# The input laid out a second time by features and normalised there, in place of transposes on TensorE

## Chip, cores and metric

One core of a Trainium2 chip runs the whole program. The metric is the device time of one execution in microseconds (us). A run's time is given as the median of several executions; the profile comes from one more execution, whose own time is given beside it. Engines are named as the profile names them: PE is TensorE's matmul side and PEld its weight loads, DVE is VectorE, ACT is ScalarE, POOL is GpSimd, SP (SPq for its queue) is SyncE, which here only issues DMAs.

## What is computed

The input x has 8 batches of 2048 tokens of 512 features. The reference, cut to what matters:

```python
    def proj(W, b):
        y = jnp.einsum('nse,fe->nsf', x, W) + b
        return y.reshape(n, s, h, d).transpose(0, 2, 1, 3)
    ...
    scores = jnp.einsum('nqhd,nkhd->nhqk', Q, K) * scale
    attn = jax.nn.softmax(scores, axis=-1)
    out = jnp.einsum('nhql,nlhd->nqhd', attn, V)
    out = out.reshape(n, s, e)
    return jnp.einsum('nse,fe->nsf', out, Wo) + bo
...
x = x + _layernorm(_L0_attn_ref(_layernorm(x, axis=-1), ...), axis=-1)
x = x + _layernorm(_L0_ffn_ref(_layernorm(x, axis=-1), ...), axis=-1)
```

By the order of the axes the attention runs, at each position, among its 16 heads of 32 features: 16 queries on 16 keys. Of the second block both kernels compute the row-wise part: a layer norm of a layer norm of x (statistics B), gain and shift (`ln_g`, `ln_b`), a layer norm (statistics C) and the residual; the contribution of its gathered attention is left out. Everything is float32, and each projection is computed with operands split in a high and a low part (`w_hi`, `w_lo`, `xT_hi`, `xT_lo`), as three products hi*hi + lo*hi + hi*lo.

## The kernel before

The tokens are cut into 128 tiles of 128 tokens (`NT`), and two tiles are a pair (`NV` = 64 pairs). All engines run the same loop over slots `s` (-4 to 135). In slot `s` PE computes, in this order: the transposes of x of tile s+1 (line 527, four 128 x 128 blocks of `xn` into the PSUM bank `ps_tv`), the scores of tile s-1 (line 554, 32 small matmul pairs), the context of tile s-2 (line 570), the projections K, Q and V of tile s (line 534, 12 matmuls each), and the output projection Y of tile s-2 (line 604). V goes into the same bank `ps_tv` that the transposes use.

There is no scheduler. The order on every engine is the order in which the lines are written, and engines wait for each other with counting semaphores.

What stands around the change:

- **x in.** SP loads `x_in` (tokens on partitions) a pair at a time. DVE takes its statistics (`x_moments`, lines 313 to 317), POOL the root of the variance (`root("X", v)`), ACT the shift (`shift("X", v)`), and ACT writes the normalised row `xn` (line 452, `normalise`). PE transposes it, ACT rounds it to the high half `xT_hi` (line 456), and DVE forms the low half `xT_lo` (line 329, `x_low`) from `ps_tv` and `xT_hi`. Feature 0 of `xn` is a constant 1, since the first row of the weights is taken out of all others and the bias stands in its place.
- **DVE in a slot.** y plus bias (353), `x_low` of tile s+1, statistics A (361; every other slot their moments), the softmax of tile s-1 (369, 371, 383, 387, 389), `kT` (396, a transpose of K out of PSUM), `pT` (403), then in odd slots the statistics B of a pair and in even slots the statistics C of a pair and those of x, then `qT` (426), and in odd slots z times gain (432).
- **POOL in a slot.** In even slots the root of A, then in every slot the softmax's last factor (266), in even slots x + residual (275), in odd slots the root of B and z + shift (282), in even slots the root of C and the output's residual (288), then the root of x.
- **ACT in a slot.** `xT_hi`, the high half of the context (480), exp (486), `xn`, in even slots the rows of A, then `v_tok` out of `ps_tv` (504), then in odd slots the rows of B into z, in even slots the rows of C into `o_sb`.
- **SP in a slot.** In odd slots the store of a pair of outputs (185), `v_key` of tile s-1 (191), read back from the DRAM scratch `v_d`, four copies `k_bd` of tile s (202), four copies `p_bd` of tile s-1 (213), then in odd slots the load of `x_in` (160), in even slots that of `res` (163), and last the store of `v_tok` of tile s into `v_d` (230). SP waits in this order: a wait that isn't met holds up every DMA behind it.

Statistics names: X for x, A, B and C for the three later layer norms. A pair costs two slots, an even and an odd one.

## Time and profile before

| | us |
|---|---|
| median of 3 runs | 1791.14 (1788.35 to 1793.31) |
| the profiled execution, its own time | 1792.47 |
| its span, as the profile shows it | 1790.9 |
| PE busy | 1720.9 (96% of the span) |
| DVE busy | 1440.6 (80%) |
| ACT busy | 850.9 (48%) |
| POOL busy | 831.5 (46%) |
| DMA, mean share of 16 engines | 54% |

The span is what the profiler's clock shows between first and last instruction; 1.6 us of the execution's own time lie outside it. A timeline row gives the start, the duration, the engine, line, operation and names; in brackets the idle time of that engine just before, and which engine's work ended it. For SPq the duration is the time that the queue took to issue the DMA, not that of the transfer.

### The profile page before, as it was taken

What the parts mean: (1) busy time and instruction counts of PE and PEld (TensorE: products, weight loads), DVE (VectorE), ACT (ScalarE), POOL (GpSimd) and SP (SyncE); (2) the same over time, 40 slices, a digit from 0 to 9 for tenths busy, and PEclk for the clock granted to TensorE, in tenths of its full rate; (3) what the DMA queues carried; (4) which work ended last, traced back from release to release, by engine and by line L of the source; (5) the groups of instructions that cost most, each with busy time, mean ns of one, the idle gap of its engine ahead of it and who ended that gap; (6) DMA issues with size and microseconds to landing.
All of it is one profiled execution on the core that took longest, in us unless ns stands there. A gap on an engine that the chain in (4) does not pass through costs nothing.

```text
span 1790.9 us, 55853 instructions
## 1 busy us (share of the span) xinstructions
PE 1720.9 (96%) x23040; PEld 1391.3 (78%) x23040; DVE 1440.6 (80%) x2824; ACT 850.9 (48%) x1800; POOL 831.5 (46%) x782
## 2 busy tenths in 40 slices
PE   4999999999999999999999999999999999999992
PEld 3778878878888788878887888788878888888771
DVE  6688878878888888878888888788878888888874
ACT  4244444445444444445444444445445445445443
POOL 1144445445444444445445444445445445445445
PEclk9999999999999999999999999999999999999996
DMA  6455555565565555555565565555565565555451
GB/s 205 106 127 136 128 146 142 127 151 138 127 153 137 126 148 142 127 138 150 126 151 134 132 152 139 125 146 145 124 147 142 129 149 136 131 148 139 116 132 59
DMA packets 361267, 244.31 MB, mean 136 GB/s; under 512 B 285875, under 2 KB 285875, under 8 KB 360502
## 3 DMA queue, kind: packets, MB, share of 16 engines
q1 hardware_dynamic: 361014, 240.75, 53.9%
q8 instruction: 182, 2.98, 0.7%
q14 instruction: 71, 0.58, 0.1%
HBM read 106.44 MB, written 67.11 MB: 97 GB/s over the span
## 4 chain that ended last, share of the span: by engine, by line
PE 95%; issue 1%; DVE 1%; POOL 1%; ACT 1%; SPq 0%; DMA 0%; POOLq 0%; ACTq 0%
PE ps_k L534 21%; PE ps_y L604 20%; PE ps_tv L534 20%; PE ps_q L534 20%; PE ps_s L554 6%; PE ps_o L570 5%; PE ps_tv L527 3%; POOL o_sb L288 0%; POOL z L282 0%; POOL x L275 0%; SPq L202 0%; DMA p_bd<-pT 0%; SPq L213 0%; ACT z L447 0%; ACT o_sb L447 0%
## 5 line engine op out<-in xcount | busy, mean ns | idle before, releaser
L266 POOL TENSOR_TENSOR probs<-probs,inv 128x512 f32<-128x512 f32 x128 | 136.0, 1062 | 396.3 <-DVE inv L389 396.3
L504 ACT ACTIVATE v_tok<-ps_tv 128x512 f32<-128x512 f32 x128 | 76.5, 597 | 500.0 <-PE ps_tv L534 500.0
L282 POOL TENSOR_TENSOR z<-z,b_row 128x512 f32<-128x512 f32 x128 | 193.1, 1529 | 226.0 <-DVE z L432 226.0
L432 DVE TENSOR_TENSOR z<-z,g_row 128x512 f32<-128x512 f32 x128 | 88.6, 692 | 169.5 <-ACT z L447 168.5
L288 POOL TENSOR_TENSOR o_sb<-o_sb,x 128x512 f32<-128x512 f32 x128 | 161.2, 1280 | 119.7 <-ACT o_sb L447 119.7
L486 ACT ACTIVATE probs<-probs 128x512 f32<-128x512 f32 x128 | 81.0, 632 | 189.2 <-DVE probs L371 189.1
L275 POOL TENSOR_TENSOR x<-x,res 128x512 f32<-128x512 f32 x128 | 163.0, 1295 | 1.7 <-ACT x L447 1.6
L534 PE MATMUL ps_k<-wk_hi,xT_hi 128*128 128x512 f32 x512 | 154.2, 423 | 3.9 <-DVE wk_lo L325 3.9
L534 PE MATMUL ps_tv<-wv_hi,xT_hi 128*128 128x512 f32 x512 | 142.0, 399 | 7.2 <-DVE xT_lo L329 7.2
L604 PE MATMUL ps_y<-wo_hi,oT_hi 128*128 128x512 f32 x512 | 141.8, 399 | 4.8 <-DVE oT_lo L376 4.8
L604 PE MATMUL ps_y<-wo_hi,oT_lo 128*128 128x512 f32 x512 | 142.4, 400 | 0.0
L534 PE MATMUL ps_k<-wk_hi,xT_lo 128*128 128x512 f32 x512 | 141.7, 398 | 0.7 <-issue 0.7
L604 PE MATMUL ps_y<-wo_lo,oT_hi 128*128 128x512 f32 x512 | 142.1, 400 | 0.0
L534 PE MATMUL ps_k<-wk_lo,xT_hi 128*128 128x512 f32 x512 | 141.0, 397 | 0.6 <-issue 0.6
L534 PE MATMUL ps_q<-wq_hi,xT_hi 128*128 128x512 f32 x512 | 140.9, 397 | 0.3 <-issue 0.3
L534 PE MATMUL ps_tv<-wv_hi,xT_lo 128*128 128x512 f32 x512 | 141.0, 397 | 0.0
L534 PE MATMUL ps_q<-wq_hi,xT_lo 128*128 128x512 f32 x512 | 140.7, 396 | 0.0
L534 PE MATMUL ps_tv<-wv_lo,xT_hi 128*128 128x512 f32 x512 | 140.7, 397 | 0.0
L534 PE MATMUL ps_q<-wq_lo,xT_hi 128*128 128x512 f32 x512 | 140.7, 396 | 0.0
L396 DVE STREAM_TRANSPOSE kT<-ps_k 128x512 f32<-128x512 f32 x128 | 138.5, 1082 | 2.7 <-PE ps_k L534 2.2
L426 DVE STREAM_TRANSPOSE qT<-ps_q 128x512 f32<-128x512 f32 x128 | 137.3, 1073 | 0.3
L480 ACT ACTIVATE oT_hi<-ps_o 128x512 fp32r<-128x512 f32 x128 | 76.6, 598 | 123.9 <-PE ps_o L570 123.9
(85 smaller groups left out, 3686.9 us busy)
## 6 DMA issues: line engine op xcount, KB each, us to landing
res<-in_xr SPq DMA_DIRECT2D x64, 512.0 KB, 4.5
k_bd<-kT SPq DMA_DIRECT2D x512, 64.0 KB, 2.0
v_d<-v_tok SPq DMA_DIRECT2D x128, 256.0 KB, 4.5
v_key<-v_d SPq DMA_DIRECT2D x128, 256.0 KB, 3.4
p_bd<-pT SPq DMA_DIRECT2D x512, 64.0 KB, 2.0
out<-o_sb SPq DMA_DIRECT2D x64, 512.0 KB, 4.9
x_in<-in_xa SPq DMA_DIRECT2D x63, 512.0 KB, 4.5
x<-in_wk SPq DMA_DIRECT2D x1, 1024.0 KB
```

The lines of the kernel that those rows point to most:

```text
L266: nc.gpsimd.tensor_tensor(probs[t % 2][:, :, :, :].rearrange("p i u k -> p (i u) k"), probs[t % 2][:, :, :, :].rearrange("p i u k -> p (i ...
L275: nc.gpsimd.tensor_tensor(x1[:, v % 3, j, :], x1[:, v % 3, j, :], res[:, v % 2, j, :], ALU.add).then_inc(x1_done, 1)
L282: nc.gpsimd.tensor_tensor(z[:, j, :], z[:, j, :], b_row[:, :], ALU.add).then_inc(z_done, 1)
L288: nc.gpsimd.tensor_tensor(o_sb[:, v % 2, j, :], o_sb[:, v % 2, j, :], x1[:, v % 3, j, :], ALU.add).then_inc(out_done, 1)
L396: nc.vector.transpose(kT[t % 2][:, :, :].rearrange("p n h -> p h n"), ps_k[:, :].rearrange("p (h d) -> p h d", d=D)).then_inc(kT_done, 1)
L426: nc.vector.transpose(qT[t % 2][:, :, :].rearrange("p n h -> p h n"), ps_q[:, :].rearrange("p (h d) -> p h d", d=D)).then_inc(qT_done, 1)
L432: nc.vector.tensor_tensor(z[:, j, :], z[:, j, :], g_row[:, :], ALU.mult).then_inc(zg_done, 1)
L486: nc.scalar.activation(probs[t % 2][:, :, :, :], probs[t % 2][:, :, :, :], ACT.Exp, scale=SCALE).then_inc(exp_done, 1)
L534: mm = nc.tensor.matmul(ps[:, :], x[:, e, :], w[:, e, :], start=x is x_hi and w is w_hi and e == 0, stop=w is w_lo and e == EC - 1)
L554: mm = nc.tensor.matmul(ps_s[32 * c:32 * c + 32, r, a * 64:a * 64 + 64], qT[t % 2][half, n:n + 2, :].rearrange("p n h -> p (n h)"), k_bd[h ...
L570: mm = nc.tensor.matmul(ps_o[32 * g:32 * g + 32, r, a * 64:a * 64 + 64], v_key[t % 2][half, 4 * g + a, :], p_bd[half, t % 2, :, 32 * n:32 ...
L604: mm = nc.tensor.matmul(ps_y[:, :], o[:, a, :], w[:, a, :], start=o is o_hi and w is wo_hi and a == 0, stop=w is wo_lo and a == EC - 1)
```

## The change

The host hands the same x over a second time, `xt`, with features on partitions. A pair of it is loaded into `x_t`, and is normalised in that layout, where the mean and the root of a token are no longer one number per partition but one per column: DVE and POOL leave them in `mr` (mean and root of the pair's tokens, one token a partition), SP stores them into the small DRAM scratch `x_d`, transposed on the way (128 x 4 single numbers), and reads them back as rows that are spread over all partitions (`mr_row`). POOL then subtracts the mean row and multiplies by the root row, in place, over 128 x 512 elements for each tile (`x_scale`). ACT puts the ones of feature 0 in and rounds to `xT_hi`, DVE forms `xT_lo` from `x_t` and `xT_hi`, both in SBUF now. `xn`, `ident`, the shift of x, and the transposes on PE are gone; V has its bank for itself.

```diff
+            def store_mr(v):
+                sp.wait_ge(root_done["X"], v + 1)
+                if v >= 2:
+                    sp.wait_ge(mr_loaded[v % 2], DMA * (v // 2))
+                sp.dma_start(x_d[v % 2].rearrange("q p -> p q"), mr[v % 2][:, :, :].rearrange("p j k -> p (j k)"),
+                             allow_slow_non_contiguous=True).then_inc(mr_stored[v % 2], DMA)
+
+            def load_mr(v):
+                sp.wait_ge(mr_stored[v % 2], DMA * (v // 2 + 1))
+                if v >= 2:
+                    sp.wait_ge(scaled_done, 2 * (v - 1))
+                sp.dma_start(mr_row[v % 2][:, :, :, :].rearrange("p j k n -> p (j k n)"),
+                             x_d[v % 2].rearrange("(a q) p -> a (q p)", a=1).broadcast_to([P, 4 * P])
+                             ).then_inc(mr_loaded[v % 2], DMA)
...
                 if s % 2 == 1:
-                    v = (s + 1) // 2 + 2
+                    v = (s + 3) // 2
+                    if 1 <= v < NV:
+                        store_mr(v)
                     if 2 <= v < NV:
-                        sp.wait_ge(xn_done, 2 * (v - 1))
-                        load_x(v)
+                        sp.wait_ge(xlo_done, 2 * (v - 1))
+                        load_xt(v)
+                    if 3 <= v + 1 < NV:
+                        sp.wait_ge(stats_done["X"], 2 * v)
+                        load_x(v + 1)
+                    if 1 <= v < NV:
+                        load_mr(v)
...
+            def x_scale(t):
+                v, j = t // 2, t % 2
+                pool.wait_ge(xt_loaded[v % 2], DMA * (v // 2 + 1))
+                pool.wait_ge(mr_loaded[v % 2], DMA * (v // 2 + 1))
+                nc.gpsimd.tensor_tensor(x_t[v % 2][:, j, :, :], x_t[v % 2][:, j, :, :],
+                                        mr_row[v % 2][:, j, 0, :].unsqueeze(1).to_broadcast([P, EC, P]), ALU.subtract
+                                        ).then_inc(centred, 1)
+                pool.wait_ge(centred, t + 1)
+                nc.gpsimd.tensor_tensor(x_t[v % 2][:, j, :, :], x_t[v % 2][:, j, :, :],
+                                        mr_row[v % 2][:, j, 1, :].unsqueeze(1).to_broadcast([P, EC, P]), ALU.mult
+                                        ).then_inc(scaled_done, 1)
...
             def x_low(t):
                 dve.wait_ge(xhi_done, t + 1)
-                nc.vector.tensor_tensor(xT_lo[t % 2][:, :, :], ps_tv[:, :].rearrange("p (c n) -> p c n", n=P),
+                nc.vector.tensor_tensor(xT_lo[t % 2][:, :, :], x_t[t // 2 % 2][:, t % 2, :, :],
                                         xT_hi[t % 2][:, :, :].bitcast(F32), ALU.subtract).then_inc(xlo_done, 1)
...
+            def x_high(t):
+                v, j = t // 2, t % 2
+                act.wait_ge(scaled_done, t + 1)
+                nc.scalar.copy(x_t[v % 2][0:1, j, 0, :], ones[:, :]).then_inc(one_put, 1)
+                act.wait_ge(one_put, t + 1)
                 if t >= 2:
+                    act.wait_ge(v_ready, t - 1)
+                nc.scalar.activation(xT_hi[t % 2][:, :, :], x_t[v % 2][:, j, :, :], ACT.Copy).then_inc(xhi_done, 1)
...
-                t = s + 1
-                if tile(t):
-                    transposes(t)
...
-    laid = {"xa": x.reshape(B, 8, 2, 4, 2, 4, 4, E).transpose(0, 1, 5, 6, 3, 4, 2, 7).reshape(NV, P, 2, E),
+    xa = x.reshape(B, 8, 2, 4, 2, 4, 4, E).transpose(0, 1, 5, 6, 3, 4, 2, 7).reshape(NV, P, 2, E)
+    laid = {"xa": xa, "xt": xa.reshape(NV, P, 2, EC, P).transpose(0, 4, 2, 3, 1),
```

The change also moves work. On DVE `x_low` goes from behind y + bias to behind `pT`. The middle of an even slot on DVE, from the transpose of K to the moments C, stood so before (`xT_lo` of the next tile is not among these rows, it stands 11 rows before the first):

```order
L396 STREAM_TRANSPOSE kT<-ps_k 128x16x32 [waits k_moved0,k_ready]
L403 STREAM_TRANSPOSE pT<-probs 128x512 [waits p_moved1,norm_done]
L415 BN_STATS stC<-z 128x6 [waits z_done] x2
L303 BN_AGGR mvC<-stC 128x2 [waits stats_doneC]
L303 BN_AGGR mvC<-stC 128x2
L308 TENSOR_SCALAR veC<-mvC 128x2 [waits aggr_doneC]
```

The same place on DVE in the changed kernel:

```order
L457 STREAM_TRANSPOSE kT<-ps_k 128x16x32 [waits k_moved0,k_ready]
L464 STREAM_TRANSPOSE pT<-probs 128x512 [waits p_moved1,norm_done]
L393 TENSOR_TENSOR xT_lo<-x_t,xT_hi 128x512 [waits xhi_done]
L479 BN_STATS stC<-z 128x6 [waits z_done] x2
L359 BN_AGGR mvC<-stC 128x2 [waits stats_doneC]
L359 BN_AGGR mvC<-stC 128x2
L364 TENSOR_SCALAR veC<-mvC 128x2 [waits aggr_doneC]
```

The subtraction of `x_low` stands between `pT` and the statistics C, and its operands are `x_t` and `xT_hi`; the statistics of x and `qT` follow behind these rows in both.

On SP, from the last copies `p_bd` of an odd slot to the first copy `k_bd` of the even slot behind it, before:

```order
L213 DMA p_bd<-pT 32x512 x3
L160 DMA x_in<-in_xa 128x1024 [waits xn_done]
L230 DMA v_d<-v_tok 128x512 [waits v_moved1,vtok_done]
L191 DMA v_key<-v_d 128x16x32 [waits o_ready,v_stored1]
L202 DMA k_bd<-kT 32x512 [waits s_ready,kT_done]
```

The same stretch of SP's queue in the changed kernel:

```order
L245 DMA p_bd<-pT 32x512 x3
L175 DMA x_d<-mr 128x4x1 [waits mr_loaded1,root_doneX]
L169 DMA x_t<-in_xt 128x1024 [waits xlo_done]
L166 DMA x_in<-in_xa 128x1024 [waits stats_doneX]
L182 DMA mr_row<-x_d 128x512 [waits scaled_done,mr_stored1]
L269 DMA v_d<-v_tok 128x512 [waits v_moved1,vtok_done]
L223 DMA v_key<-v_d 128x16x32 [waits o_ready,v_stored1]
L234 DMA k_bd<-kT 32x512 [waits s_ready,kT_done]
```

One load became four DMAs: the store of the means, two loads and the load of the rows, which waits for that store. The store of `v_tok`, the load `v_key` and `k_bd` stand behind that wait.

On POOL, an even slot from the root of A on, before:

```order
L238 TENSOR_TENSOR rsA<-veA,minus_half 128x2 [waits var_doneA]
L266 TENSOR_TENSOR probs<-probs,inv 128x512 [waits inv_done]
L275 TENSOR_TENSOR x<-x,res 128x512 [waits lny_done,r_loaded1]
L275 TENSOR_TENSOR x<-x,res 128x512 [waits lny_done]
L238 TENSOR_TENSOR rsC<-veC,minus_half 128x2 [waits var_doneC]
L288 TENSOR_TENSOR o_sb<-o_sb,x 128x512 [waits lnz_done] x2
L238 TENSOR_TENSOR rsX<-veX,minus_half 128x2 [waits var_doneX,xn_done]
```

The same slot on POOL in the changed kernel:

```order
L277 TENSOR_TENSOR rsA<-veA,minus_half 128x2 [waits var_doneA]
L317 TENSOR_TENSOR probs<-probs,inv 128x512 [waits inv_done]
L287 TENSOR_TENSOR x_t<-x_t,mr_row 128x512 [waits mr_loaded0,xt_loaded0]
L291 TENSOR_TENSOR x_t<-x_t,mr_row 128x512 [waits centred]
L277 TENSOR_TENSOR rsC<-veC,minus_half 128x2 [waits var_doneC]
L340 TENSOR_TENSOR x<-x,res 128x512 [waits lny_done,r_loaded1]
L340 TENSOR_TENSOR x<-x,res 128x512 [waits lny_done]
L346 TENSOR_TENSOR o_sb<-o_sb,x 128x512 [waits lnz_done] x2
L281 TENSOR_TENSOR mr<-veX,minus_half 128x2 [waits var_doneX]
```

The two operations of `x_scale` follow the softmax's factor directly, and the root of C now comes ahead of x + residual. At the start, `store_mr` and `load_mr` of pair 0 stand between the weight loads; DVE forms the low half of wo later, in slot 0, and POOL no longer waits for the rows `bo`, `ln_g` and `ln_b` before the loop.

## Rows read from the trace of the kernel before

**Rows 1.** The page: span, busy times, the chain that ended last by engine.

```profile
span 1790.9 us, 55853 instructions
PE 1720.9 (96%) x23040; PEld 1391.3 (78%) x23040; DVE 1440.6 (80%) x2824; ACT 850.9 (48%) x1800; POOL 831.5 (46%) x782
PE 95%; issue 1%; DVE 1%; POOL 1%; ACT 1%; SPq 0%; DMA 0%; POOLq 0%; ACTq 0%
```

**Rows 2.** Timeline of PE over one pair: start, duration, engine, line, operation.

```profile
804.10 0.86 PE L554 MATMUL ps_s<-k_bd,qT 64*32 64x64 f32 x64
...
816.88 0.60 PE L527 MATMUL ps_tv<-ident,xn 128*128 128x128 f32 x4
817.41 0.86 PE L554 MATMUL ps_s<-k_bd,qT 64*32 64x64 f32 x64
...
830.72 0.86 PE L554 MATMUL ps_s<-k_bd,qT 64*32 64x64 f32 x64
```

**Rows 3.** Timeline of PE: scores of tile 2 and of tile 127.

```profile
64.12 0.86 PE L554 MATMUL ps_s<-k_bd,qT 64*32 64x64 f32 x64
...
1743.96 0.86 PE L554 MATMUL ps_s<-k_bd,qT 64*32 64x64 f32 x64
```

**Rows 4.** Timeline of DVE, POOL and ACT: an even slot, then the next odd slot.

```profile
804.35 0.68 DVE L353 TENSOR_TENSOR x<-ps_y,bo_row 128x512 f32<-128x512 f32 x1
...
810.25 1.06 POOL L266 TENSOR_TENSOR probs<-probs,inv 128x512 f32<-128x512 f32 x1 [2.62 <-DVE inv L389]
...
811.35 0.71 DVE L403 STREAM_TRANSPOSE pT<-probs 128x512 f32<-128x512 f32 x1 [0.17 <-POOL probs L266]
...
815.43 1.08 DVE L426 STREAM_TRANSPOSE qT<-ps_q 128x512 f32<-128x512 f32 x1
...
827.58 0.60 ACT L504 ACTIVATE v_tok<-ps_tv 128x512 f32<-128x512 f32 x1 [4.85 <-PE ps_tv L534]
...
829.66 1.40 DVE L432 TENSOR_TENSOR z<-z,g_row 128x512 f32<-128x512 f32 x2 [2.39 <-ACT z L447]
```

**Rows 5.** Groups by line: shapes, count, busy us, mean ns, idle before.

```profile
L282 POOL TENSOR_TENSOR z<-z,b_row 128x512 f32<-128x512 f32 x128 | 193.1, 1529 | 226.0 <-DVE z L432 226.0
L275 POOL TENSOR_TENSOR x<-x,res 128x512 f32<-128x512 f32 x128 | 163.0, 1295 | 1.7 <-ACT x L447 1.6
...
L329 DVE TENSOR_TENSOR xT_lo<-ps_tv,xT_hi 128x512 fp32r<-128x512 f32 x128 | 87.9, 687 | 32.4 <-ACT xT_hi L456 32.4
```

**Rows 6.** Timeline of SP's queue: end of an odd slot and the even slot.

```profile
803.04 0.58 SPq L160 DMA_DIRECT2D x_in<-in_xa  x1
803.72 0.40 SPq L230 DMA_DIRECT2D v_d<-v_tok  x1
808.26 0.37 SPq L191 DMA_DIRECT2D v_key<-v_d  x1
811.20 2.42 SPq L202 DMA_DIRECT2D k_bd<-kT  x4
813.72 2.43 SPq L213 DMA_DIRECT2D p_bd<-pT  x4
```

**Rows 7.** The page's DMA issues: KB each, median us to landing.

```profile
v_key<-v_d SPq DMA_DIRECT2D x128, 256.0 KB, 3.4
p_bd<-pT SPq DMA_DIRECT2D x512, 64.0 KB, 2.0
```

**Rows 8.** Landing times of line 230, `v_d<-v_tok`, over all tiles.

```profile
DMA to landing us min/median/max: 2.1/4.5/6.1
```

**Rows 9.** One window: engines' busy times, TensorE clock, DMA share, GB/s.

```profile
806.25:807.25 1.00, 1.00 (x6) 0.80 (x5) 0.95 (x4) 0.00 (x0) 0.89 (x2) 1.00 0.97 381
```

**Rows 10.** Waits of PE: in total, times, longest.

```profile
PE ps_o L570 <- issue: 10.8, 14, 2.6
```

**Rows 11.** Timeline at the start and in the tail.

```profile
34.29 2.49 SPq L202 DMA_DIRECT2D k_bd<-kT  x4
...
1775.75 0.70 POOL L238 TENSOR_TENSOR rsB<-veB,minus_half 128x2 f32<-128x2 f32 x1
```

170 lines of the change are left out of this document (89 added, 81 removed).

## The prediction

> **What bounds the kernel now.** First the chain that ended last: PE holds 95% of it, and PE is busy 96% of the span, DVE 80% [rows 1]. So PE's own stream sets the time, and one pair is the unit to count in. The timeline of PE gives it: scores start at 804.10, 817.41 and 830.72, 13.31 us a slot and 26.62 a pair, and each slot holds one set of transposes, 0.53 us from its start to the scores behind it [rows 2]. Over the whole run it is a little more: from the scores of tile 2 to those of tile 127 there are 125 slots in 1679.84 us [rows 3], 13.44 each, 26.88 a pair. The excess over 26.62 is 16 us in all, and 10.8 of them are waits of the context matmuls (line 570) in 14 slots [rows 10]; those wait for the copies `p_bd`.
>
> Then the question what is late next when PE gives up 0.53 us a slot. The timeline of DVE answers it. In an odd slot DVE has spare time: it waits 2.39 us for ACT's z, and ACT can't be earlier, since it first takes `v_tok`, for which it waits until PE has finished V, 4.85 us of waiting [rows 4]. In an even slot DVE then works through without a gap that counts, from y + bias at 804.35 to the end of `qT` at 816.51 [rows 4], and the scores of the next slot need that `qT`. Today PE's transposes cover the last of it: the scores start at 817.41, 0.9 us after `qT` is done.
>
> **Part by part.** *PE.* 128 sets of transposes go, 0.53 us each: 68 us, all on the path. Without a new wait a pair would be 26.62 - 1.06 = 25.56 us.
>
> *The DVE loop.* One closed chain runs through both slots of a pair. From the scores of an odd slot (817.41) it goes through the projections, `v_tok`, the rows of B and z times gain, which ends at 829.66 + 1.40 = 831.06: 13.65 us [rows 2, 4]. From there DVE's even slot, 816.51 - 804.35 = 12.16 us [rows 4], and then the next odd slot's scores. Sum 25.81 us. In the kernel before it hides below 26.62; with 25.56 on PE it is what is left. `x_low` only changes its place in it and keeps its 0.69 us [rows 5]; xn leaves ACT, but ACT's part of this chain starts at `v_tok`, which PE sets, so nothing is won there.
>
> *x_low beside POOL.* What is new is that `x_low` reads two operands in SBUF while POOL works through SBUF as well. The groups by line show what such a meeting costs on POOL's side: z + shift takes 1529 ns on average, x + residual, same shape and operation, 1295 [rows 5]. The first of each two z + shift starts while DVE is at its second z times gain, an instruction with both operands in SBUF, and 0.47 us a pair is about what then is left of that one. So the two don't run side by side. In the changed kernel `x_low` comes just behind `pT`, and POOL's subtraction just behind the softmax's factor. By the timeline the factor ends at 811.31 and `pT` at 812.06 [rows 4]; the subtraction, at 1.29 us by the row of x + residual [rows 5], lasts until 812.60. If the one that comes second waits, `x_low` waits 0.54 us. If POOL's operation is as short as the factor, 1.06 us [rows 4], it is 0.31; if DVE is never held, 0. I take 0.54, since the operands are two full tensors as those of x + residual are. No row shows DVE held: there it came first. The loop becomes 25.81 + 0.54 = 26.35 us. In the odd slot the same wait falls into the 2.39 us of spare time.
>
> The Trainium skill, SBUF — State Buffer, section "Who interferes with whom", says that a DVE instruction with two SBUF inputs contends with a GpSimd instruction that reads SBUF, and that "Issue order, not op shape, decides who blocks". The stretched z + shift agrees with it; the half in which DVE is the one held is shown by no row of this trace. With the page's rule the pair is 26.35 us, without it 25.81.
>
> *POOL.* Added are 256 operations of 1.06 to 1.29 us, 270 to 330 us beside 831.5 busy now [rows 1, 4, 5]; 1160 of some 1770 leave room. In an even slot POOL has the factor, the two of `x_scale`, the roots, x + residual and output + residual: the last of these ends some 17 us after the even slot's scores, and the next factor is due at about 18. That is 0.8 us of cover; if POOL is later than that, the next odd slot's `pT` moves, which has DVE's spare time behind it. Cost taken: 0.
>
> *ACT.* xn and the shift of x go, a copy of 128 numbers and the same rounding out of SBUF come: ACT is busy 48% [rows 1]. Cost 0; it is covered by ACT's wait for `v_tok` [rows 4].
>
> *SP and the DMAs.* This is the part that no row shows. Before, the load of x is issued at 803.04 and the store of `v_tok` at 803.72, and the load `v_key`, which waits for that store, at 808.26: 5.2 us from the first to the last [rows 6]. A store of `v_tok` alone lands in 2.1 us, behind a load in 4.5 [rows 8], so bytes ahead of it in the rings count. Now 768 KB more go ahead of it, and SP waits for the store of the means. The bytes: at the 381 GB/s of the busiest stretch [rows 9] 2.1 us; by the difference of 2.4 us for 512 KB in rows 8 up to 3.6 us. So 7.8 to 9.3 us from the store of the means to `v_key`, with an issue of 0.5 us in front. The store of the means is 512 single numbers. Its landing is bounded below by a `p_bd` copy (2.0 us) and above by `v_key` with its 2048 pieces of 128 bytes (3.4 us) [rows 7]; I take 3, nearer to the pieces. Then the load of the rows and the store of `v_tok` leave at about 4.1 us, and the last lands before the bytes are through. So the wait hides behind the bytes.
>
> Does `v_key` then hold up `k_bd`? Counted from an odd slot's scores: `kT` is done 5.7 us in (6.85 from y + bias to the issue of `k_bd` in an even slot [rows 4, 6], less 0.69 of `x_low` and 0.5 of A's moments), eight copies are issued in 4.95 us [rows 6], the four DMAs and the wait take 7.8 to 9.3, `v_key` 0.4, and `k_bd` may go at 18.8 to 20.4. `kT` of the even slot is done at 12.8 + 7.0 = 19.8. So it is hidden or 0.6 us late, and the copies `p_bd` have 0.8 us of cover: their last one lands 13.4 us into the even slot, and the context needs it 0.7 us after the scores that now start at 13.57. Cost taken 0. As a loop of its own this is 24.5 to 26.0 us a pair.
>
> *Waits for p_bd.* Their cover is 0.3 us larger than before (the slot is 13.57 instead of 13.31 us, and `kT` is 0.1 us earlier in it). The 16 us of excess come from some 35 slots; with 0.3 off each, about 8 us stay.
>
> *Start and tail.* `k_bd` of tile 0 is issued at 34.29 [rows 11], now behind the store and load of the rows of pair 1: 3 us later. In the tail the root of C comes ahead of x + residual, and the root of B at 1775.75 [rows 11] comes about 2 us earlier. Net +1.
>
> **The sum.** 62.5 pairs at 26.35 us are 1646.9, plus 8 is 1654.9, against 1679.8: -24.9. With +1 for start and tail the profiled execution, 1792.47 us, would be 1768.6; the median of the runs is 1.3 below the profiled one, so 1767 us.
>
> **Rivals.** *No collision:* DVE and POOL run side by side, or the wait is 0.3 us. 25.81 a pair, with all 16 us of excess since the slot is shorter: 62.5 x 25.81 + 16 = 1629, so 1741 us (1756 with the short wait). For it: no DVE row is ever stretched. Against it: z + shift.
>
> *DVE held twice:* `x_low` does not get in between POOL's subtraction and multiplication and waits for both. That is 1.29 us more in the loop, 27.64 a pair: 62.5 x 27.64 + 4 = 1731.5, 1844 us, slower than before. It decides from a wait of 26.88 - 25.81 = 1.07 us on. For it: POOL's instructions follow each other without a gap. Against it: the multiplication waits for the semaphore of the subtraction, and DVE is then already waiting.
>
> *The queue:* the four DMAs and the wait take so long that SP's loop (16.7 us a pair beside them) sets the pace. From 9.6 us on it costs something, from 10.2 it is slower than before; for that the store of 512 single numbers would have to take some 7 us. At 11 us it is 27.7 a pair, 1847 us. For it: everything behind it in SP's order is on the path, and `p_bd` already is late now and then [rows 10]. Against it: the bounds from rows 7.
>
> The Trainium skill, DMA: Bandwidth & Descriptors, section "Specifications", has pieces under 512 B done as read-modify-write. It gives no duration for it, and no row here has pieces of 4 bytes; it speaks for this rival.
>
> *Nothing to measure:* fuller rings make more late copies, and these eat what the loop gives: 1786 to 1796 us.
>
> **Chances.** Forecast (1755 to 1780) 0.45; no collision or a short one 0.25; held twice 0.08; the queue 0.12; nothing to measure 0.10. Faster by over 0.3% (what a measurement of this kernel can tell) 0.70, within 0.3% 0.10, slower 0.20. The range leaves out the two slow rivals: 1736 to 1798.
>
> **What would show it.** Right: no transposes; a pair of 26.3 us; PE waiting some 0.8 us before the scores of odd slots, for DVE's `qT`; `xT_lo` at about 1.2 us instead of 0.69 (or an idle gap in front of it), in even and odd slots alike. Wrong: `xT_lo` at 0.69 us and a pair of 25.8 (no collision), at over 2 us (held twice); `k_bd` in even slots issued over 1 us after `kT`, and PE waiting at the context of even tiles (the queue).

## The result and the profile after

The changed kernel is slower: 2502.91 us (2491.15 to 2505.24) against 1792.22 us (1788.35 to 1793.63) beside it, a ratio of 1.3957 (95% interval 1.3907 to 1.4007). The forecast was 1767 us, in a range of 1736 to 1798. The profiled execution took 2504.05 us.

The page of the kernel after: span, busy times, the chain that ended last by engine, the rows of two groups, and the landings (last number, median us).

```profile
span 2502.3 us, 55078 instructions
PE 1857.7 (74%) x22528; PEld 1460.3 (58%) x22528; DVE 1515.3 (61%) x2824; ACT 741.8 (30%) x1608; POOL 1162.8 (46%) x1035
...
PE 56%; issue 20%; DMA 11%; DVE 5%; SPq 4%; another core or an unknown queue 2%; ACT 1%; POOL 1%; POOLq 0%; DVEq 0%; ACTq 0%
...
L618 PE MATMUL ps_o<-p_bd,v_key 64*32 64x64 f32 x8192 | 145.5, 256 | 333.4 <-issue 321.7
L287 POOL TENSOR_TENSOR x_t<-x_t,mr_row 128x512 f32<-128x512 f32 x128 | 167.6, 1309 | 305.4 <-DMA mr_row<-x_d 305.4
...
x_t<-in_xt SPq DMA_DIRECT2D x64, 512.0 KB, 13.8
v_d<-v_tok SPq DMA_DIRECT2D x128, 256.0 KB, 5.3
x_in<-in_xa SPq DMA_DIRECT2D x63, 512.0 KB, 14.5
```

Against [rows 1], PE is no longer what fills the span: it has fewer instructions (the transposes are gone) and yet is busy 137 us longer, and idle for 645 us instead of 70. POOL is busy as long as the forecast said (1163 us, forecast 1160), so its work is as it was costed. What changed is the DMAs, which with SP and "issue" now hold a third of the chain: the load of x lands after 14.5 us (4.5 in the kernel before), and the rows of means and roots keep POOL waiting for 305 us. `xT_lo` takes 871 ns on average and not the 1.2 us of the forecast: POOL is often still waiting for its rows when DVE comes to it.

SP's own waits, in total us, times and longest:

```profile
SPq L182 <- DMA x_d<-mr: 559.4, 59, 12.1
SPq L223 <- DMA v_d<-v_tok: 555.2, 128, 7.3
```

SP spends 559 us, 9.5 at a time, waiting for the store of the means, 2 KB in 512 pieces of 4 bytes. The timeline of SP shows one pair (start, duration, engine, line, operation):

```profile
1203.96 0.53 SPq L175 DMA_DIRECT2D x_d<-mr  x1
1204.53 0.53 SPq L169 DMA_DIRECT2D x_t<-in_xt  x1
1205.10 0.43 SPq L166 DMA_DIRECT2D x_in<-in_xa  x1
1214.48 0.33 SPq L182 DMA_DIRECT2D mr_row<-x_d  x1
1214.91 0.38 SPq L269 DMA_DIRECT2D v_d<-v_tok  x1
1222.31 0.37 SPq L223 DMA_DIRECT2D v_key<-v_d  x1
1222.78 3.07 SPq L234 DMA_DIRECT2D k_bd<-kT  x4
```

The store goes at 1203.96, the load of its rows at 1214.48: 10.52 us, where the forecast had 4.1 with the issues. Behind that the store of `v_tok` waits for the bytes of the two loads, another 7.40 us, so `v_key` leaves 18.35 us after the store of the means and not 7.8 to 9.3. Over the whole run the way from the store of the means to `v_key` is 18.2 us in the median. `kT` was done at 1219.46 and its copies start 3.3 us later.

The view of windows has the other half. Columns: length, busy us of PE, PE's loads, DVE, ACT and POOL, then TensorE's granted clock, the busy share of the DMA engines and GB/s.

```profile
1205.00:1213.00 8.00, 2.70 (x106) 1.89 (x105) 4.95 (x9) 1.97 (x4) 3.68 (x3) 0.83 0.90 32
1211.00:1217.00 6.00, 3.87 (x35) 3.02 (x36) 1.83 (x4) 3.05 (x7) 0.50 (x1) 0.50 0.49 27
```

From 1205 to 1213 the DMA engines are 90% busy and move 32 GB/s; in [rows 9] they moved 381 at 97%. What they are busy with shows in the view of the DMAs, for the stretch that begins half a microsecond later (packets, bytes; then packets, MB and busy share of the queue):

```profile
DMA packets 62, 0.25 MB, mean 34 GB/s; under 512 B 0, under 2 KB 0, under 8 KB 62
q1 hardware_dynamic: 62, 0.25, 92.9%
```

None of the 4-byte pieces is among these packets: in the packet records they are over by 1205.5, at 7 to 9 ns each. The 62 are 4-KB packets of the loads behind them, and these take 1.8 us each on average and up to 10.2. So the time isn't spent where the small pieces are recorded; all the DMA engines are slow behind them, which is more than the order of one queue. And PE itself stops, in the middle of 64 context matmuls that have no wait between them:

```profile
1206.78 0.48 PE L618 MATMUL ps_o<-p_bd,v_key 64*32 64x64 f32 x33
...
1210.43 0.43 PE L618 MATMUL ps_o<-p_bd,v_key 64*32 64x64 f32 x4 [3.16 <-issue]
...
1213.13 0.71 PE L618 MATMUL ps_o<-p_bd,v_key 64*32 64x64 f32 x27 [2.27 <-issue]
...
1213.78 2.07 PE L586 MATMUL ps_k<-wk_hi,xT_hi 128*128 128x512 f32 x4
```

Behind such a stop the granted clock is 0.50, the 1.2 GHz level, and four K matmuls take 2.07 us. The page's groups of projections, in the order in which they run (K first, Q behind it; mean ns of one in front of the idle time), show that only what stands behind the context is slow:

```profile
L586 PE MATMUL ps_k<-wk_hi,xT_hi 128*128 128x512 f32 x512 | 219.9, 569 | 39.3 <-DVE xT_lo L393 30.2
...
L586 PE MATMUL ps_k<-wk_hi,xT_lo 128*128 128x512 f32 x512 | 186.9, 499 | 11.0 <-issue 11.0
...
L586 PE MATMUL ps_k<-wk_lo,xT_hi 128*128 128x512 f32 x512 | 162.1, 443 | 14.2 <-issue 14.2
...
L586 PE MATMUL ps_q<-wq_lo,xT_hi 128*128 128x512 f32 x512 | 143.1, 402 | 16.0 <-issue 16.0
```

In the kernel before, K's first group took 423 ns:

```profile
L534 PE MATMUL ps_k<-wk_hi,xT_hi 128*128 128x512 f32 x512 | 154.2, 423 | 3.9 <-DVE wk_lo L325 3.9
```

Against the 402 ns of Q's last group, K's three groups are 512 times 167, 97 and 41 ns longer, 156 us; against K's own groups in the kernel before it is 132 us. With 37 us more for the context, 9 for the scores and 11 for the other projections it outweighs the 78 us of the transposes that are gone, and PE is busy longer. (Groups overlap a little, so these don't add up to the 137 us exactly.) From the starts of the scores in the timeline, the median pair is 38.15 us long, against the 26.62 of [rows 2].

### The profile page after: what moved, and what is told of

It is laid out like the page before. It is cut to its first block, busy times and chain, and to the rows that moved or that the text cites. A ratio compares the mean times of both kernels' runs of the same rounds, so it can differ in the third digit from the quotient of the medians.

```text
span 2502.3 us, 55078 instructions
## 1 busy us (share of the span) xinstructions
PE 1857.7 (74%) x22528; PEld 1460.3 (58%) x22528; DVE 1515.3 (61%) x2824; ACT 741.8 (30%) x1608; POOL 1162.8 (46%) x1035
## 3 DMA queue, kind: packets, MB, share of 16 engines
q8 instruction: 178, 2.92, 0.5%
## 4 chain that ended last, share of the span: by engine, by line
PE 56%; issue 20%; DMA 11%; DVE 5%; SPq 4%; another core or an unknown queue 2%; ACT 1%; POOL 1%; POOLq 0%; DVEq 0%; ACTq 0%
PE ps_k L586 17%; PE ps_q L586 11%; PE ps_v L586 10%; PE ps_y L650 9%; DMA x_in<-in_xa 5%; PE ps_o L618 5%; PE ps_s L602 4%; DMA x_d<-mr 3%; SPq L234 2%; SPq L245 1%; DMA v_d<-v_tok 1%; DVE stX L372 1%; DVE qT L490 1%; DVE kT L457 1%
## 5 line engine op out<-in xcount | busy, mean ns | idle before, releaser
L618 PE MATMUL ps_o<-p_bd,v_key 64*32 64x64 f32 x8192 | 145.5, 256 | 333.4 <-issue 321.7
L566 ACT ACTIVATE v_tok<-ps_v 128x512 f32<-128x512 f32 x128 | 76.5, 598 | 889.5 <-PE ps_v L586 884.6
L618 PEld LDWEIGHTS ps_o<-p_bd,v_key 64*32 64x32 f32 x8192 | 113.0, 120 | 353.9 <-issue 353.0
L287 POOL TENSOR_TENSOR x_t<-x_t,mr_row 128x512 f32<-128x512 f32 x128 | 167.6, 1309 | 305.4 <-DMA mr_row<-x_d 305.4
L437 DVE TENSOR_TENSOR oT_lo<-ps_o,oT_hi 128x512 fp32r<-128x512 f32 x128 | 88.2, 689 | 358.8 <-ACT oT_hi L548 358.7
L602 PE MATMUL ps_s<-k_bd,qT 64*32 64x64 f32 x8192 | 118.8, 239 | 177.7 <-issue 149.6
L586 PE MATMUL ps_k<-wk_hi,xT_hi 128*128 128x512 f32 x512 | 219.9, 569 | 39.3 <-DVE xT_lo L393 30.2
L602 PEld LDWEIGHTS ps_s<-k_bd,qT 64*32 64x32 f32 x8192 | 96.8, 112 | 226.9 <-issue 220.8
L291 POOL TENSOR_TENSOR x_t<-x_t,mr_row 128x512 f32<-128x512 f32 x128 | 175.5, 1371 | 10.0
L586 PEld LDWEIGHTS ps_k<-wk_hi,xT_hi 128*128 128x128 f32 x512 | 122.7, 265 | 76.5 <-DVE xT_lo L393 30.2
L586 PEld LDWEIGHTS ps_k<-wk_hi,xT_lo 128*128 128x128 f32 x512 | 134.9, 264 | 49.2 <-issue 11.5
## 6 DMA issues: line engine op xcount, KB each, us to landing
x_in<-in_xa SPq DMA_DIRECT2D x63, 512.0 KB, 14.5
```

Of the source, the lines that this page charges most:

```text
L287: nc.gpsimd.tensor_tensor(x_t[v % 2][:, j, :, :], x_t[v % 2][:, j, :, :], mr_row[v % 2][:, j, 0, :].unsqueeze(1).to_broadcast([P, EC, P]), ...
L291: nc.gpsimd.tensor_tensor(x_t[v % 2][:, j, :, :], x_t[v % 2][:, j, :, :], mr_row[v % 2][:, j, 1, :].unsqueeze(1).to_broadcast([P, EC, P]), ...
L586: mm = nc.tensor.matmul(ps[:, :], x[:, e, :], w[:, e, :], start=x is x_hi and w is w_hi and e == 0, stop=w is w_lo and e == EC - 1)
L602: mm = nc.tensor.matmul(ps_s[32 * c:32 * c + 32, r, a * 64:a * 64 + 64], qT[t % 2][half, n:n + 2, :].rearrange("p n h -> p (n h)"), k_bd[h ...
L618: mm = nc.tensor.matmul(ps_o[32 * g:32 * g + 32, r, a * 64:a * 64 + 64], v_key[t % 2][half, 4 * g + a, :], p_bd[half, t % 2, :, 32 * n:32 ...
```

## The experiments

Each kernel was measured beside runs of the kernel before (1788.8 to 1790.8 us in median); ratios are against those. The first question: is it the store, and what about it?

**The pieces four times as long.** The changed kernel, with the means stored as 128 pieces of 16 bytes; POOL then reads the rows with a stride of four numbers.

```diff
-sp.dma_start(x_d[v % 2].rearrange("q p -> p q"), mr[v % 2]...)
+sp.dma_start(x_d[v % 2], mr[v % 2]...)          # x_d is (2, P, 4)
-mr_row[v % 2][:, j, 0, :]
+mr_row[v % 2][:, :, j, 0]
```

> The changed kernel, but the store of means and roots goes as 128 pieces of 16 bytes (each partition's four numbers stay together in the scratch), and POOL picks its row out of the spread tile with a stride of four numbers. All bytes, waits and their order stay. Theory (the single pieces are the cost): in the changed kernel 10.5 us pass from the issue of the store (1203.96) to the issue of the load that waits for it (1214.48); that falls below 4 us, x_t lands in under 6 us instead of 13.8, and the pair comes to 26 to 27 us: 1740 to 1810 us. Rival (the 768 KB more per pair and the longer queue are the cost): the store's wait stays over 8 us and the time over 2300 us.

Measured: 1906.99 us, ratio 1.0659 (1.0613 to 1.0705). 596 of the 711 us go with the pieces, now four times as long and a quarter as many. The rest is more than was expected: 1907 us lies over the 1740 to 1810 of the theory, though far under the rival's 2300, so something else costs as well. The timeline shows the queue again, the odd slot's DVE and POOL ahead of it:

```profile
913.48 1.57 POOL L286 TENSOR_TENSOR x_t<-x_t,mr_row 128x512 f32<-128x512 f32 x1
...
914.29 1.31 DVE L392 TENSOR_TENSOR xT_lo<-x_t,xT_hi 128x512 fp32r<-128x512 f32 x1
...
919.00 0.53 SPq L175 DMA_DIRECT2D x_d<-mr  x1
...
920.64 0.34 SPq L181 DMA_DIRECT2D mr_row<-x_d  x1
...
921.08 0.38 SPq L268 DMA_DIRECT2D v_d<-v_tok  x1
...
928.36 0.37 SPq L222 DMA_DIRECT2D v_key<-v_d  x1
```

Now the load of the rows follows directly: the store had landed when SP came to it. From the store to `v_key` are 9.36 us (9.67 in the median of the run), the upper end of the forecast's 7.8 to 9.3, and most of them are the bytes ahead of the store of `v_tok`. `xT_lo` starts while POOL's subtraction runs and takes 1.31 us instead of 0.69: it ends 0.55 us after that subtraction, which itself ends at 915.05. So the held `x_low` is there too, in the size forecast; in the even slot behind this one it ends 0.54 us after the subtraction.

**The wait moved.** The changed kernel with its 512 pieces, the load of the rows behind the `v_key` of the next slot, so that SP doesn't stop ahead of the store of `v_tok`.

```diff
-                    if 1 <= v < NV:
-                        load_mr(v)          # ahead of the store of v_tok
+                v = (s + 2) // 2
+                if s % 2 == 0 and 1 <= v < NV:
+                    load_mr(v)              # behind v_key
```

> The changed kernel with the 512 single-number pieces as they are; the load of the rows, and with it SP's wait for the store, is moved behind the v_key load of the next slot, so that the store of v_tok and v_key don't stand behind that wait. If SP's waiting is what costs, the pair falls from some 38 us to below 29, 1950 us or less. If the pieces block the DMA rings themselves, x_t and x_in still land in about 14 us, v_d takes 10 us and more in odd slots instead of 5.3 (it is now queued behind the pieces), and the time stays over 2200 us.

Measured: 2442.35 us, ratio 1.3653 (1.3619 to 1.3688). Almost nothing comes back. SP's wait is gone and stands one step further on, `SPq L223 <- DMA v_d<-v_tok` is now 829.4 us (68 of them, up to 14.4) where it was 555.2, and the two loads of x still land after 12.2 and 12.9 us. Whatever is behind the pieces on the DMA engines is late, wherever SP waits. This run alone doesn't prove that the wait costs nothing, since the rows now leave later too, and POOL waits for them for 652 us instead of 305; the next run leaves both out.

**The store alone.** The kernel before, with nothing of the change but a store of 512 numbers per pair, from `g_row` into an unread array, ahead of the load of x.

```diff
+                        sp.dma_start(x_d[v % 2].rearrange("q p -> p q"), g_row[:, 0:4], ...)
                         load_x(v)
```

> The kernel before with one thing added: ahead of each load of x from pair 2 on, a store of 128 x 4 single numbers (the first four of g_row, never read again) into a scratch in DRAM, in 512 pieces of 4 bytes as in the change. Nobody waits for it except the store two pairs later. Theory (the pieces block the rings): x_in lands in about 14 us instead of 4.5, the store of v_tok behind it likewise, and the time is 2050 to 2500 us. Rival (only SP's wait on it costs): 1790 to 1810 us, x_in at 4.5 to 6 us.

Measured: 2253.7 us, ratio 1.2599 (1.2551 to 1.2646): 465 us for 62 stores of 2 KB, 7.5 us each. Nothing waits for this store but the one two pairs later, and still the load of x lands after 12.1 us. Its timeline has PE's stops as well, in the slot behind the store as above:

```profile
848.06 0.49 PE L577 MATMUL ps_o<-p_bd,v_key 64*32 64x64 f32 x31
...
854.10 0.77 PE L577 MATMUL ps_o<-p_bd,v_key 64*32 64x64 f32 x32 [3.77 <-issue]
```

and its waits hold `PE ps_o L577 <- issue: 233.8, 76, 8.0` for the 10.8 us of [rows 10]. PE's stops need neither POOL's new work nor the rows.

**The same store, its pieces apart.** Still 512 pieces of 4 bytes; only their distance in DRAM changes, by a longer last axis of the unread array.

```diff
+    x_d = nc.dram_tensor("x_d", (2, P, 4, 128), ...)     # 512 bytes apart; 16: 64 bytes
+                        sp.dma_start(x_d[v % 2][:, :, 0], g_row[:, 0:4], ...)
```

> As the kernel before with the unread store of 512 single numbers, but each number goes to an address 512 bytes from the next. If it is the number of pieces that costs, the time is that of the store into neighbouring addresses (within 3%). If it is that neighbouring 4-byte pieces, written by different DMA engines, get in each other's way, x_in lands in under 7 us and the time is below 1850 us.

Measured: 1791.14 us, ratio 1.0013 (1.0003 to 1.0024). As many packets as in the run above (394004 in both pages), as many bytes, and 463 us less. So the cost is neither the number nor the shortness of the pieces by itself: it is that pieces as short as these are written beside each other. Two more distances:

> The kernel before with the unread store of 512 single numbers, each 64 bytes from the next (at neighbouring addresses it took 2254 us, at 512 bytes 1791 us). If what hurts is pieces that share a stretch of 64 bytes, 1785 to 1800 us; if the stretch is larger than 64 bytes, 1850 us and more.

Measured, 64 bytes apart: 1795.9 us, ratio 1.0039 (1.0023 to 1.0055).

> The same store, each number 16 bytes from the next, so that four share 64 bytes. If sharing 64 bytes is what hurts, the time lies between the two: 1830 to 2100 us; if only directly neighbouring numbers hurt, 1785 to 1800 us.

Measured, 16 bytes apart: 1833.93 us, ratio 1.0247 (1.0227 to 1.0268).

In these three runs a number's neighbours in memory come mostly from its own partition (four to a partition), in the changed kernel always from the neighbouring partitions. So the distance and the order were changed together, and three more kernels take them apart. The order of the changed kernel, at a distance of 64 and of 16 bytes:

```diff
+    x_d = nc.dram_tensor("x_d", (2, 4, P, 16), ...)      # 64 bytes apart; 4: 16 bytes
+                        sp.dma_start(x_d[v % 2][:, :, 0].rearrange("q p -> p q"), g_row[:, 0:4], ...)
```

> The kernel before with the unread store of 512 pieces of 4 bytes, in the order of the changed kernel (neighbours in memory come from neighbouring partitions), but 64 bytes apart instead of side by side. If the distance decides: about 1796 us, as in the run with the pieces 64 bytes apart whose neighbours come from one partition. If it decides that neighbours come from different partitions: 2254 us again.

> The same order, neighbours from neighbouring partitions, 16 bytes apart. If only the distance decides: 1834 us, as with neighbours from one partition. If the order has a part in it below 64 bytes: clearly over 1834, up to 2254 us.

Measured: 1790.46 us, ratio 1.0005 (0.9995 to 1.0016), and 1801.53 us, ratio 1.0076 (1.0052 to 1.0101). The second is below both expectations, which started at 1834. And the other order with the numbers side by side, read from SBUF 16 bytes apart so that they stay single:

```diff
+    x_d = nc.dram_tensor("x_d", (2, P, 4), ...)
+                        sp.dma_start(x_d[v % 2], g_row[:, 0:16].rearrange("p (a b) -> p a b", b=4)[:, :, 0], ...)
```

> The unread store with four numbers of a partition side by side in memory, as in the 16-byte version, but read from SBUF 16 bytes apart, so that they can't be one piece of 16 bytes. If short pieces side by side are slow whoever writes them: 2254 us or thereabouts. If only neighbours from different partitions are slow: 1791 to 1834 us, since here three of four neighbours come from the same partition.

Measured: 2106.12 us, ratio 1.1780 (1.1718 to 1.1842), between the two expectations and nearer to the first.

| distance of the 4-byte pieces | neighbours from | time, us | us per store | load of x lands after, us |
|---|---|---|---|---|
| side by side | other partitions | 2253.7 | 7.50 | 12.1 |
| side by side | the same partition | 2106.12 | 5.11 | 9.7 |
| 16 bytes | the same partition | 1833.93 | 0.72 | 5.8 |
| 16 bytes | other partitions | 1801.53 | 0.19 | 4.9 |
| 64 bytes | the same partition | 1795.9 | 0.11 | 4.9 |
| 64 bytes | other partitions | 1790.46 | 0.02 | 4.6 |
| 512 bytes | the same partition | 1791.14 | 0.04 | 4.7 |

("Us per store" is the difference to the kernel before of the same comparison, over 62 stores.) The distance decides, in either order; who the neighbour is counts for less, and with either sign. The 0.02 and 0.04 us per store are hardly to be told from nothing. The 128 pieces of 16 bytes of the first experiment fit in: they lie side by side too, but their starts are 16 bytes apart, as in the two rows that cost little.

The Trainium skill, DMA: Bandwidth & Descriptors, section "Specifications", has pieces under 512 bytes done as read-modify-write. That pieces beside each other would then have to follow one another fits the table, but no run here shows the mechanism. Size alone doesn't set the price: at a distance of 64 or 512 bytes 4-byte pieces cost 0.4% at most (interval up to 0.55%).

**What is left of the change without the slow store.** From the 16-byte version on, the other terms of the forecast can be seen one by one. First the order on SP: the store of `v_tok` ahead of the four DMAs.

```diff
+                t = s
+                if tile(t): ...  sp.dma_start(v_d[t % 2], v_tok[t % 2][:, :])
                 if s % 2 == 1:
                     store_mr(v); load_xt(v); load_x(v); load_mr(v)
-                t = s
-                if tile(t): ...  sp.dma_start(v_d[t % 2], v_tok[t % 2][:, :])
```

> The kernel with 16-byte pieces, and in every slot the store of v_tok is issued ahead of the loads of x, xt, the rows and the residual instead of behind them. In the 16-byte kernel 9.4 us pass from the store of means (919.00) to v_key (928.36), and k_bd of the even slot waits for it (928.83). Theory (what is left of the loss is the store of v_tok lying behind 1.25 MB in the rings): v_d lands in 2 to 3 us instead of 5.7, k_bd follows kT directly in even slots, the pair falls from 28.4 to 26.4 to 27.2 us: 1770 to 1820 us. Rival (the loss is x_low and POOL holding each other up): the pair stays above 27.8 us, over 1865 us.

Measured: 1845.69 us, ratio 1.0315 (1.0292 to 1.0339), 61 us less than with the bytes ahead, and over the 1770 to 1820 expected. SP's wait for `v_d` falls from 517.7 us in all to 10.7. What stood ahead of the store of `v_tok` was thus not hidden: the forecast had given it a cost of 0. Not all of the 61 us are the change's own bytes, since the move also takes that store from behind SP's wait for the means (32.8 us in all) and, in even slots, from behind the load of `res`, where it stood in the kernel before too.

**x_low behind the moments.** On top of that, `x_low` moved behind the moments of B and of C, where POOL's subtraction and multiplication are over or nearly so.

```diff
-                t = s + 1
-                if 1 <= t < NT: x_low(t)             # behind pT
                 ...                                  # moments of B or C, epsilon, shift
+                t = s + 1
+                if 1 <= t < NT: x_low(t)
                 v = (s + 4) // 2
                 if s % 2 == 0 and 1 <= v < NV: x_moments(v)
```

> As the kernel with v_tok's store first, and x_low moved on DVE from behind pT to behind the moments of B and C, where POOL's two operations on x_t are over. In the 16-byte kernel xT_lo takes 1.3 to 1.8 us there instead of 0.69. Theory (the two engines don't run two-operand SBUF work side by side): xT_lo is back at 0.69 us on average, POOL's multiplication falls from 1.87 to about 1.5 us, and the even slot of DVE is 0.6 to 1.1 us shorter: 1740 to 1775 us. Rival (no collision; xT_lo is slow because of its SBUF operands): xT_lo stays above 1.2 us and the time is that of the kernel with v_tok's store first within 0.5%.

Measured: 1818.68 us, ratio 1.0160 (1.0142 to 1.0177), 27 us less, and over the 1740 to 1775 expected. Three groups by line of this kernel (busy us, mean ns of one, then the idle time before them):

```profile
L392 DVE TENSOR_TENSOR xT_lo<-x_t,xT_hi 128x512 fp32r<-128x512 f32 x128 | 88.6, 693 | 4.0 <-ACT xT_hi L521 4.0
L363 DVE TENSOR_SCALAR veC<-mvC 128x2 f32<-128x2 f32 x64 | 53.8, 841 | 2.5 <-DVE mvC L358 0.4
L365 DVE TENSOR_SCALAR veB<-mvB 128x2 f32<-128x2 f32 x64 | 53.3, 832 | 2.2
```

`x_low` is back at its undisturbed 0.69 us (1235 ns on average in the kernel above), but the collision didn't vanish, it moved: the additions of epsilon of C and B, two numbers per partition, now stand where `x_low` stood and take 841 and 832 ns on average instead of 491 and 170; an undisturbed one takes 170. Those of A, X and C were held in the changed kernel already (738, 407 and 402 ns), and the forecast doesn't mention them. There POOL adds the shift to z just as DVE comes to epsilon of A; the timeline of the kernel after:

```profile
1206.26 2.98 POOL L331 TENSOR_TENSOR z<-z,b_row 128x512 f32<-128x512 f32 x2 [3.75 <-DVE z L498]
...
1208.53 0.73 DVE L364 TENSOR_SCALAR veA<-mvA 128x2 f32<-128x2 f32 x1
```

POOL's two additions end at 1209.24 and DVE's `veA` at 1209.26: it waited for them. Its mean is 738 ns in the kernel after and 306 in the one before, where it came later relative to z.

The Trainium skill, SBUF — State Buffer, section "Who interferes with whom", names `tensor_scalar` among the operations that can take the shared ports and says that "Issue order, not op shape, decides who blocks". These rows agree: an operation on two numbers is held as long as a full one.

**The additions of epsilon on POOL.** On top of that, epsilon of A, C and X is added by POOL, just ahead of its root; DVE keeps B's.

```diff
+                if k in "AC":
+                    pool.wait_ge(aggr_done[k], 2 * (v + 1))
+                    nc.gpsimd.tensor_scalar(ve[k][:, :], mv[k][:, :, 1], EPS, None, ALU.add)...
```

> The kernel with v_tok's store first and x_low late (1819 us), with the three additions of epsilon for A, C and X (tensor_scalar over two numbers) moved from DVE to POOL. There veA takes 0.75, veC 0.84 and veX 0.25 us, against 0.31, 0.30 and 0.17 in the kernel before. Theory (DVE's even slot is what a pair waits for, and these tiny operations are held by POOL's operations on SBUF): the even slot of DVE is 1.5 to 2 us shorter, PE's waits for qT (60 us now) fall below 20 us: 1745 to 1785 us. Rival (they only stand where DVE would wait anyway): within 0.3% of the kernel it starts from.

Measured: 1805.11 us, ratio 1.0085 (1.0068 to 1.0102), 14 us less, and over the 1745 to 1785 expected. POOL's wait for the rows has grown from 82.5 to 133.5 us meanwhile.

**The rows earlier.** On top of that, the store of the means ahead of the copies `p_bd` in odd slots, and the load of the rows ahead of the two loads of x.

```diff
+                v = (s + 3) // 2
+                if s % 2 == 1 and 1 <= v < NV: store_mr(v)
                 t = s - 1
                 if tile(t): ...                      # the four copies p_bd
...
-                    store_mr(v); load_xt(v); load_x(v); load_mr(v)
+                    load_mr(v); load_xt(v); load_x(v)
```

> As the kernel with the epsilons on POOL, and the 16-byte store of means and roots is issued ahead of the copies p_bd of odd slots and the load of the rows ahead of the loads of x. In the kernel with x_low late the rows land 6.2 us after their issue, and POOL waits 82 us for them in 53 slots. Theory: these waits are gone, SP doesn't wait for the store any more, 10 to 30 us less than the kernel with the epsilons on POOL. Rival: POOL has time for them, no difference beyond 0.3%.

Measured: 1795.43 us, ratio 1.0026 (1.0012 to 1.0040), 10 us less, the low end of the 10 to 30 expected. The store of 16-byte pieces now lands in 1.6 us in median, POOL's wait for the rows falls from 133.5 us to 17.1. This is the best version. The last one has `x_low` back behind `pT`:

```diff
+                if 1 <= s + 1 < NT: x_low(s + 1)      # behind pT
...
-                if 1 <= s + 1 < NT: x_low(s + 1)      # behind the moments
```

> As the kernel with the rows early, but x_low goes back to its place in the change, directly behind pT, where POOL is at its first operation on x_t. Theory (0.5 to 0.9 us of waiting per slot, in even slots on the path): xT_lo 1.2 to 1.4 us on average and 20 to 50 us more than with x_low late. Rival (without the small operations DVE has time to spare): the same within 0.3%.

Measured: 1798.09 us, ratio 1.0045 (1.0031 to 1.0060), which the two intervals don't tell apart from the version above. The expected 20 to 50 us aren't there. DVE is held in either order: with `x_low` later it takes 1063 ns on average and B's addition 752, with `x_low` back they take 1303 and 170. No version is faster than the kernel before.

The version with 1795.43 us is closest to what the forecast had in mind. PE's timeline over one of its undisturbed pairs, and DVE's operations in front of the scores of the odd slot:

```profile
459.56 0.86 PE L608 MATMUL ps_s<-k_bd,qT 64*32 64x64 f32 x64
...
468.78 1.45 DVE L399 TENSOR_TENSOR xT_lo<-x_t,xT_hi 128x512 fp32r<-128x512 f32 x1
...
471.75 1.09 DVE L496 STREAM_TRANSPOSE qT<-ps_q 128x512 f32<-128x512 f32 x1
...
472.89 0.86 PE L608 MATMUL ps_s<-k_bd,qT 64*32 64x64 f32 x64 [0.42 <-DVE qT L496]
...
485.72 0.86 PE L608 MATMUL ps_s<-k_bd,qT 64*32 64x64 f32 x64
```

13.33 and 12.83 us, 26.16 a pair, with PE waiting for DVE's `qT` ahead of the odd slot: the loop that the forecast put at 26.35, though with epsilon's additions taken out of it. But over the whole run a pair is 26.89 us (from the scores of tile 2 at 70.44 to those of tile 127 at 1750.99 are 125 slots), as long as the 26.88 before [rows 3]. Where the gain goes shows in PE's waits (us in total, times, longest) and, from its timeline, in one such place:

```profile
PE ps_o L624 <- issue: 36.9, 42, 4.1
PE ps_s L608 <- DVE qT L496: 16.8, 46, 0.4
```

```profile
283.74 0.86 PE L608 MATMUL ps_s<-k_bd,qT 64*32 64x64 f32 x64 [0.41 <-DVE qT L496]
...
285.98 1.05 PE L624 MATMUL ps_o<-p_bd,v_key 64*32 64x64 f32 x64 [1.38 <-issue]
286.96 2.07 PE L592 MATMUL ps_k<-wk_hi,xT_hi 128*128 128x512 f32 x4
...
299.55 0.86 PE L608 MATMUL ps_s<-k_bd,qT 64*32 64x64 f32 x64
```

The context matmuls come 1.38 us late, the four K matmuls behind them take the 2.07 us of the lower clock, and the slot is 15.81 us long. Of such waits there are 42 with 36.9 us, against 14 with 10.8 us before [rows 10]. The DMA engines have more to do in the same time, the windows from 65 to 1745 of the kernel before and of this one:

```profile
65.00:1745.00 1680.00, 1669.63 (x22502) 1352.14 (x22492) 1380.57 (x2724) 811.19 (x1729) 795.54 (x739) 1.00 0.56 137
```

```profile
65.00:1745.00 1680.00, 1624.39 (x21999) 1292.50 (x21998) 1432.18 (x2540) 712.58 (x1543) 1255.83 (x1169) 1.00 0.63 166
```

0.63 instead of 0.56 of the time, 166 instead of 137 GB/s: x is loaded twice. That the fuller DMA engines make the copies late is the likely reason, but no run tests it by itself.

## Why the prediction was wrong

**The step that failed: "The store of the means is 512 single numbers. Its landing is bounded below by a `p_bd` copy (2.0 us) and above by `v_key` with its 2048 pieces of 128 bytes (3.4 us) [rows 7]; I take 3".** It took 10.5 us to where SP went on. `v_key` was no upper bound: it has more pieces, but none of them shorter than 128 bytes, and how short pieces written side by side behave no row of the trace before showed. A transfer of another shape was taken for the upper end of the range, and 3 us, "nearer to the pieces", for the value. The runs show what it costs: 596 us of the 711 come from 512 pieces of 4 bytes in place of 128 of 16.

**"So the wait hides behind the bytes."** It didn't, for a second reason: the loads behind the pieces are slow on all DMA engines. The wait and the bytes were taken to run side by side; in the trace they add up, 10.5 and 7.4 us.

**The queue rival** had the direction and half of the mechanism (a slow store, and everything behind it on the path), a chance of 0.12 and too small a price. It named 7 us for the store as the point from which the kernel is slower, and took 11 us in all for its example; measured are 18.35. Its own formula, SP's loop of 16.7 us and the total, gives 35.1 us a pair with that, 38.15 were measured. For the missing 3 us it had no term. PE's stops within a block and the K matmuls at the 1.2 GHz level behind them are the likely ones: K's 132 us are 2.1 a pair. Its sign to look for was met: copies `k_bd` 3.3 us after `kT`, and PE waiting at the context, though partly inside the block.

**The bytes, 7.8 to 9.3 us:** nearly right in size (9.67 in the median with 16-byte pieces), wrong in cost. "Hidden or 0.6 us late" was costed at 0; taking the store of `v_tok` out from behind them gave 61 us, in part by the two side effects named there. Its range reached 0.6 us a pair past the cover, some 37 us in the run, and the sum took none of it.

**PE, 68 us for the transposes:** nearly right. Where nothing waits, the odd slot is 12.83 us instead of 13.31 (12.78 forecast), which would be 61 us for 128 slots.

**x_low beside POOL, 0.54 us:** right, it takes 1.24 to 1.32 us on average where it stands behind `pT`, 0.55 to 0.63 more than 0.69, and the example above ends 0.55 us behind POOL. Moving it away gave 27 us; 62.5 times 0.54 are 34. The forecast's "No row shows DVE held", and under the rivals "no DVE row is ever stretched", were misreadings of the trace. In the kernel before, the addition of epsilon of A already waits for POOL:

```profile
803.81 3.02 POOL L282 TENSOR_TENSOR z<-z,b_row 128x512 f32<-128x512 f32 x2 [3.37 <-DVE z L432]
806.55 0.30 DVE L308 TENSOR_SCALAR veA<-mvA 128x2 f32<-128x2 f32 x1
```

POOL's two additions end at 806.83 and `veA` at 806.85, 0.30 us long where the undisturbed `veX` of that slot takes 0.17. The row was there to show both that DVE can be held and that two numbers are enough.

**The DVE loop, 25.81 us:** incomplete. By the same rule as `x_low`, the additions of epsilon in the even slot were held: 755 instead of 306 ns for A, 491 instead of 300 for C, 417 instead of 172 for X (the kernel with the store of `v_tok` first), together 0.89 us. With them, 26.35 becomes 27.2 us, and that kernel has a median pair of 27.51. The forecast looked only for operations with two full operands. With this term alone, and no slow store, the forecast would have been 62.5 x 0.89 = 55 us higher, some 1822 us, slower than before. That all of it is on the path is not shown: taking three of the four additions from DVE gave 14 us, with POOL doing them instead.

**POOL, cost 0:** right for its busy time, but the stretch in which POOL works on SBUF is what DVE meets, and 256 full operations made that stretch longer.

**Waits for p_bd, "about 8 us stay":** wrong. In the version with 1795.43 us the run is 45 us longer than 62.5 undisturbed pairs of 26.16. The late copies take more than the longer slot gives; that the fuller DMA engines cause them is likely, not shown. The rival "nothing to measure" (0.10) had said so: 1786 to 1796 us, and this is where the mended change ends.

**Start and tail, +1:** +3.8 in that version. The scores of tile 2 are at 70.44 instead of 64.12 [rows 3], since POOL must scale x ahead of the first K, which starts at 24.68 instead of 18.21; from the scores of tile 127 to the end are 44.4 instead of 46.9 us.

## What to carry to other kernels

A DMA's price is not bounded by another one with more pieces: where a change brings a shape of transfer that the trace doesn't show, pieces of a few bytes written side by side above all, measure it alone before anything rests on it, or give the case "it holds up all other DMAs" a real chance. When an engine gets more work on SBUF, list every DVE operation that falls beside it, the smallest too, because one on two numbers waits as long as one on 512. And a stream that was bounded by an engine 96% busy, with the loops of DVE and SP 1 to 2 us a pair behind it, gives back little: here 68 us of PE work went, and those loops and the copies were waiting behind it.

## What the runs showed of the hardware

- Behind 512 pieces of 4 bytes written to neighbouring addresses the DMA engines were slow for some 10 us: 32 GB/s at a busy share of 0.90, with 4-KB packets of other DMAs of up to 10.2 us, while the pieces themselves are recorded at 7 to 9 ns each. A store of that kind, which no engine's work waited for, cost 7.5 us in a kernel; with its pieces 16 bytes apart 0.19 to 0.72 us, and 64 bytes apart 0.02 to 0.11.
- A DVE operation on 2 numbers per partition, 170 ns when undisturbed, took 1.02 us beside POOL in the kernel after (`veC` at 1222.06), and 841 ns on average in one version. In the kernel before, `veA` took 306 ns on average.
- PE stopped inside a row of 64 matmuls without a wait between them, for 3.16 and 2.27 us in the example, while the DMA engines were held; such waits (the first matmul of a block included, which can wait for a late copy) make 322 us at the context and 150 at the scores. Counted in the trace, some 200 us of them, in 49 places, are inside a block; in the kernel before there is none. Not settled is why. The page counts two instruction queues on the same DMA engines, 2.92 and 0.61 MB, which is 64 bytes for each of the 55078 instructions; so it may be that PE's next instructions were late, and these blocks use them up fastest, the 64 scores with their 64 weight loads in 0.69 us, from 1206.09 to 1206.78. Against it stands that no packet of these queues is recorded in the stretch from 1205 to 1213. No run here separates the two.

The row for this last point, from the page's DMA queues (packets, MB, share of 16 engines):

```profile
q8 instruction: 178, 2.92, 0.5%
q14 instruction: 76, 0.61, 0.1%
```
